# A three-layer pointwise MLP: one ScalarE instruction for three PSUM banks, and VectorE's first activation three depths ahead

## The reference

```python
f = _lrelu(_conv1x1(x, sw1, sb1)); f = _lrelu(_conv1x1(f, sw2, sb2)); f = _conv1x1(f, sw3, sb3)
feat = concat([broadcast(f over D=128 depths), pts], axis=1)     # 17 channels
h = _lrelu(_conv1x1(feat, mw1, mb1))      # 32
h = _lrelu(_conv1x1(h, mw2, mb2))         # 32
h = _lrelu(_conv1x1(h, mw3, mb3))         # 16
x = x + sigmoid(_conv1x1(h, mw4, mb4))    # one value per pixel and depth
```

## Time and profile before

| | |
|---|---|
| median of three runs | 9058.28 us |
| profiled execution | 9065.39 us, span 9063.6 us |
| busy share of the span | PE 96%, VectorE 95%, ScalarE 91%, GpSimd 64% |
| layer 1 | from about 5880 us to the end, 128 chunks |
| `leaky2` on ScalarE (L982) | 2048 instructions, 1968.7 us |
| `leaky1` on VectorE (L1279) | 1024 instructions, 2360.8 us |

### The profile page before, as it was taken

The page is one execution under the profiler, slowest core; times in us unless marked ns, Lnnn a source line. Parts: engine busy times, 40 slices in busy tenths (PEclk is TensorE's granted clock), DMA queues, the critical chain, the costliest instruction groups (busy, mean ns, idle before and its releaser), DMA issues. The chain is left out here.

```text
span 9063.6 us, 447466 instructions
## 1 busy us (share of the span) xinstructions
PE 8683.7 (96%) x199698; PEld 3689.6 (41%) x199698; DVE 8638.8 (95%) x7296; ACT 8216.6 (91%) x13813; POOL 5797.7 (64%) x2710
## 2 busy tenths in 40 slices
PE   7999999999999999999999999899999999999999
PEld 4555555555555555555555555422222222222221
DVE  6999999999999999999999999999999999999999
ACT  6888888888888988898899898799999999999999
POOL 6999999999999999999999999800000000000000
PEclk9999999999999999999999999999999999999999
DMA  3333333333333333333333333211111111111100
GB/s 117 97 97 93 87 86 85 98 99 98 85 86 83 99 97 97 88 86 85 85 86 85 85 86 86 83 29 24 22 24 24 23 22 24 24 22 26 20 13 14
DMA packets 375774, 605.32 MB, mean 67 GB/s; under 512 B 95824, under 2 KB 96562, under 8 KB 373346
## 3 DMA queue, kind: packets, MB, share of 16 engines
q1 hardware_dynamic: 352320, 541.43, 22.0%
q0 software_dynamic: 19040, 34.26, 2.7%
q10 hardware_dynamic: 2498, 1.00, 0.0%
HBM read 236.58 MB, written 71.30 MB: 34 GB/s over the span
## 5 line engine op out<-in xcount | busy, mean ns | idle before, releaser
L1207 DVE TENSOR_TENSOR_SCAN arena<-arena,carried,ps 128x512 f32<-128x512 f32 x3968 | 4753.5, 1260 | 229.9 <-PE ps L513 216.2
L1041 POOL TENSOR_TENSOR arena<-arena 128x1024 f32<-128x1024 f32 x2048 | 4796.2, 2376 | 129.4 <-PE ps L524 81.7
L871 ACT ACTIVATE arena<-arena,a_neg 128x512 f32<-128x512 f32 x4096 | 2677.9, 712 | 6.4
L513 PE MATMUL ps<-arena 64*32 64x128 f32 x131072 | 2317.6, 275 | 48.1 <-DVE arena L1207 31.5
L1279 DVE SCALAR_TENSOR_TENSOR arena<-arena,neg_p 128x2048 f32<-128x2048 f32 x1024 | 2360.8, 2346 | 0.7 <-ACT arena L947 0.7
L513 PEld LDWEIGHTS ps<-arena 64*32 64x32 f32 x131072 | 1840.0, 106 | 1191.4 <-DVE arena L1207 657.9
L982 ACT ACTIVATE arena<-ps,b2t 128x1024 f32<-128x1024 f32 (+1 forms) x2048 | 1968.7, 1024 | 132.0 <-PE ps L695 128.7
L1087 POOL DMA_DIRECT2D out<-arena x128 | 110.9, 866 | 3073.0 <-ACT arena L994 2999.4
L695 PE MATMUL ps<-arena,w2s 32*32 32x512 f32 x32768 | 1388.5, 601 | 102.7 <-ACT arena L982 79.6
L988 ACT ACTIVATE arena<-ps,bm 128x1024 f32<-128x1024 f32 x1024 | 1167.4, 1140 | 3.5 <-PE ps L708 3.5
L708 PE MATMUL ps<-arena,m 64*32 64x512 f32 x16384 | 1136.3, 601 | 3.5 <-ACT arena L988 0.9
(11 more groups left out here) (140 smaller groups left out, 6027.0 us busy)
## 6 DMA issues: line engine op xcount, KB each, us to landing
arena<-arena SPq DMA_DIRECT2D x4096, 64.0 KB, 2.0
arena<-c_d SPq DMA_DIRECT2D x1024, 128.0 KB, 3.2
xr<-in_x SPq DMA_DIRECT2D x128, 256.0 KB, 3.2
out<-xr SPq DMA_DIRECT2D x128, 256.0 KB, 3.3
xs<-out SPq DMA_DIRECT2D x128, 256.0 KB, 2.9
out<-arena POOLq DMA_DIRECT2D x128, 256.0 KB, 4.0
xs<-in_x SPq DMA_DIRECT2D x96, 256.0 KB, 3.1
arena<-in_x SPq DMA_DIRECT2D x4, 2048.0 KB, 18.2
```

The costliest lines, as they stand in the source:

```text
L513: k = mm(dst, du_t[i % 2][64 * r:64 * r + 64, c, 32 * e:32 * e + 32], diag[gp][64 * r:64 * r + 64, c, j, :], start=True, stop=True)
L871: A(dA[(UNITS * t + m) % DR][:, gi, :], drep[:, e, :], ACT.Exp, scale=a_neg[:, e, 2 * gp + gi:2 * gp + gi + 1]).then_inc(s_dA, 1)
L1041: nc.gpsimd.tensor_tensor(hc[m % CR], H[:, m % HR, :, :], crep[:, 2 * gp:2 * gp + 2, :], ALU.mult).then_inc(s_ch, 1)
L1207: V.tensor_tensor_scan(H[:, m % HR, gi, :], dA[(UNITS * t + m) % DR][:, gi, :], dbu[m % 2].rearrange("p (l g) -> p g l", g=2)[:, gi, :], 0 ...
```

## The change

In shared depths ScalarE's two instructions (banks 0 and 1, then bank 2) become one of 1536 elements. It waits for both halves of mm2, and counts `s_t2` up by two at its end. VectorE issues `leaky1` three depths ahead. TensorE's stream is the same as before.

```diff
+            def leaky2_three(t, n, k):
+                act.wait_ge(s_m2, t * (2 * NG) + (2 * k + 2))
+                act.wait_ge(s_m3, t * NG + (k - 3))
+                if t == 1 and k == 2:
+                    act.wait_ge(s_ch, UNITS * (NT + 1))
+                bias = point(n, k)
+                A(t2[k % 4][:, 0:3, :], m2_ps[:, 0:3, :], ACT.Prelu, bias=b2t[:, bias:bias + 1], alpha=SLOPE).then_inc(s_t2, 2)
+
             def leaky2(t, n, k, half):
...
-                last, bias = 3 if half == 1 and k in SHARED else 2 * half + 2, point(n, k)
+                last, bias = 2 * half + 2, point(n, k)
...
-                    leaky2(t, n, k, 0)
-                    leaky2(t, n, k, 1)
+                    if k in SHARED:
+                        leaky2_three(t, n, k)
+                    else:
+                        for half in range(2):
+                            leaky2(t, n, k, half)
...
-                    if k + 2 < NG:
-                        leaky1(i, k + 2)
+                    if k + 3 < NG:
+                        leaky1(i, k + 3)
                     elif ahead:
-                        leaky1(i + 1, k + 2 - NG)
+                        leaky1(i + 1, k + 3 - NG)
...
-            for k in range(2):
+            for k in range(3):
                 leaky1(0, k)
```

## The result

The changed kernel takes 9172.78 us (four runs, 9166.63 to 9182.47); the kernel before, on the same chip, 9057.49 (9043.78 to 9060.74). The ratio is 1.0129, with a 95% interval of 1.0117 to 1.0141: slower by 115 us, between 106 and 128. The forecast was 9167.

A forecast was written before the change was run, and what follows sets the result against it. A closed loop between TensorE and ScalarE over four banks was taken to lead, VectorE close behind. 16 x 6.28 + 0.72 + 0.75 = 101.95 us per four chunks, 3.40 over 98.55; times 32, 109 more: 9167 us, range 9085 to 9245.

The forecast's parts named there:

- ScalarE's issue leads: Rival: ScalarE sets layer 1's pace, so the 0.13 us saved in each of 512 pairs counts fully; 8991 us, chance 0.09.
- No change: Rival: ScalarE's 0.34 us of idle time takes the lost overlap, the merged instruction returns the rest; 9058 us, chance 0.06.
- the slope: ScalarE's instruction lengths: 512 elements take 695 ns, 1024 take 1134, so 512 more cost 439; merged instruction 1.56 us.
- TensorE's own loop is shorter: Step on layer 1's pair: TensorE's loop takes 6.17 us against 6.28 through ScalarE, so ScalarE's waits set the pace.
- the other loop: Loop through ScalarE's merged instruction, its two halves of the unshared depth and mm2's late second half; 6.28 us a pair.
- TensorE's loop alone counts: Rival: mm2's second half is not late, so a pair takes 6.17 us; 9114 us, chance 0.12.
- The extras: Sigmoids and feature layers in four chunks of layer 1: 0.18 us each, 0.72 together, and 0.25 each, 0.75 together.
- Three ahead: VectorE's first activation three depths ahead: removes TensorE's 5.9 us of waits, at most 7 over the stage; counted as nothing.
- The waits of ScalarE: ScalarE's waits for TensorE's mm2 (L695) were to grow from 96 us in 2800 to some 320.

The follow-up runs named there:

- Late start alone: Kernel before, two instructions kept, but the first of a shared depth waits for both halves of mm2; 9128.07 us, ratio 1.0072.
- late release alone: Kernel before, two instructions kept, but in shared depths only the end of the second gives the banks back to TensorE; 9180.84 us, ratio 1.0134.
- the kernel in which TensorE's loop is shorter: Changed kernel with TensorE's wait for VectorE's bias (s_hb) ahead of mm2's first half, not between the halves; 9173.05 us, ratio 1.0132.

## Why the prediction was right, and what in it was not

*The mechanism* held: merging removes the overlap by halves, on both sides of the instruction, and a new wait of ScalarE appears ahead of the depth that is not shared. Late start alone and late release alone each cost time with no instruction merged. The rival "ScalarE's issue leads" (8991) failed as its condition said it would: mm2's second half comes later than ScalarE is free, and the 55 us that the shorter instruction is worth are less than either wait takes. "No change" failed because the idle time does not take the late start up: late start alone cost 69 us, and the wait of L990, 0.32 in the pair shown, is new.

Grouping two instructions raised TensorE's wait for ScalarE from 0.24 to 0.80 in a pair. With this the trace agrees with the second of the two rules of the Trainium skill (Perfetto Trace Analysis, Optimizing Scalar/DVE Operations) that the prediction weighed, by which, if an engine is not saturated but causes bubbles on others, breaking up its instructions may let work be completed sooner.

*The size*: 109 us were forecast, 115 came by the medians, 126 by the stage. Term by term, for the pair shown: restart 0.14 (0.14 forecast), first half seen 1.19 (1.20), two halves 2.12 (2.13), second half started and seen 1.31 (0.05 + 1.20), merged instruction 1.54 (1.56). Sum 6.30 against 6.28. Two errors of opposite sign hide in it:

- The second half was 0.06 late. 0.05 of that is the merged instruction's own delay: it starts that much after VectorE's add, which waits for the same half, and with a count of one the delay is gone.
- The merged instruction was 0.02 shorter than the slope gave.

The pair shown is one of the shorter ones: those of the depths 4 and 6 take 6.355 on average, 0.075 above the forecast. (Before, they took 6.12, and not the 6.06 of the chain that I used.) Four chunks take 102.33 on average and not 101.95, and took 98.40 and not 98.55: 0.38 and 0.15, times 32, are the 17 us between forecast and stage.

*The step that failed* is "TensorE's own loop is shorter: 6.17, so TensorE no longer sets the pace, ScalarE's waits do". TensorE's loop takes 6.30, and it still leads, if only just, in most pairs that have neither sigmoid nor feature layer. In the terms of the chain above, mm2 behind its wait takes 1.27 where I had put 1.10, mm3 1.02 (1.09), mm4 0.99 (0.99), the next mm2 until the merged instruction starts 1.34 (1.29), that instruction 1.55 (1.56), the restart 0.14: 6.31. The term that was mis-sized is mm2. I took it from a chain in which it did not wait; behind a wait its two halves don't follow each other closely, because a second wait stands between them, and with that one ahead of both, mm3 started 1.08 after mm2 and not 1.21. That ScalarE's waits set the pace was wrong for these pairs too: the second half starts late, as forecast, but VectorE's add, in 160 of the 186 such pairs in which it waited for that half, follows mm2's start by the same 1.35 or 1.36 as before. With a feature layer it does so in fewer than half of the pairs, so ScalarE's waits count there. That the forecast came out so close is in part luck: the other loop, which I did size, has nearly the same length. The rival "TensorE's loop alone counts", 9114, was out because I had made that loop too short, not for the reason that I gave; late release alone, which has no late second half, cost 122.

*The extras* were about right. From the step of one L981 to the next: a pair with a sigmoid takes 6.455 on average (forecast 6.46), one with a feature layer 6.45 (6.53).

*Three ahead*: nothing, as forecast, alone and with the merge (9181.1 without, 9172.78 with, their ratios' intervals nearly the same).

*The waits of ScalarE* add up to 121.4 + 107.4 = 229 in 2800 us, not to some 320. This was an error of my bookkeeping: I took waits from start to start, and the profile counts idle time from the end of an instruction, which lies about 0.1 behind the next start when two follow each other (1.14 long, 1.00 apart). VectorE waits in most pairs, as forecast, and its share is 94.3%. The granted clock stayed at 1.00.

## What to carry to other kernels

An instruction that reads several banks of a buffer without a second copy has two prices besides its own length: it starts when the last bank is written, and gives the first bank back when it is through with the last. Before merging such instructions, follow one period of each closed loop through the buffer, with the merged start and the merged end; if no loop gets shorter, the instruction's saving is paid for twice. And size every loop, not only the one that you expect to lead, with durations from rows in which the instruction had waited, since two loops that nearly tie hide each other from an edit to one of them. That the steps of a loop add up to the period does not show that it leads, since the steps of any path from one start to the next do. Ask of each step if it is longer than where nothing holds it up.

## What the runs showed of the hardware

- An instruction that counts its semaphore up by two started 0.05 us after another engine's that waited for the same event, with "issue" as the profile's releaser; counting by one, both started at the same time (7005.08). In the compiled kernel the first has its waits on a separate semaphore instruction ahead of it, the second carries one itself.
- Where several waits stand ahead of one instruction, their order matters: with the late one on TensorE's weight load itself, mm2 restarted 0.04 us after the merged instruction's end, and 0.14 with it on a separate instruction. In 512 pairs 0.1 is 51 us if it lies on the loop; on the kernel before, where it doesn't, the same order gave nothing (ratio 1.0001).
- mm2's 32 matmuls, restarted after a wait, took 1.15 us when no wait stood between their halves, and 1.27 to 1.36 with one there, although what it waits for was done (in the changed kernel VectorE's add ended at 7024.57, and mm2 restarted at 7025.55).
- mm2's second half was seen by VectorE 1.36 us after mm2's start when it started 0.07 after the first half (kernel before), 1.35 when it started 0.14 after it (changed kernel), and 1.42 when it started 0.23 after it (the kernel in which TensorE's loop is shorter).
- ScalarE's 1536 elements take 1546 ns on average, 512 more than 1024 (1112) cost 434.
